# AdaLN attention with a mixture-of-experts FFN on one core: the last unit's chain ordered by hand among the rounds of the group before it, and one copy of k issued later

## The reference

```
x: (2, 1024, 128) f32; 16 heads of 8; one shared k and v of 8 columns; 16 experts, top 4
sa, ca, ga, sb, cb, gb = six slices of silu(c) @ wmod, per batch
h = layernorm(x) * (1 + ca) + sa
x = x + ga * (softmax(causal(q k^T / sqrt(8))) v) @ w_proj      # q, k, v = h @ w_attn
h = layernorm(x) * (1 + cb) + sb
g = sigmoid(h @ gate_w^T); combine = the top 4 of g, divided by their sum, 0 elsewhere
hin, vin = h @ e_win[e], h @ e_vin[e]           # 16 experts of width 64
routed = sum_e (silu(hin) * vin * combine[e]) @ e_wout[e]
shared = (silu(h @ ws_in) * (h @ vs_in)) @ ws_out
x = x + gb * (shared + routed)
```

## Time and profile before

| | us |
|---|---|
| median of 3 runs | 406.76 (405.55 to 408.6) |
| the profiled execution, its own time | 406.49 |
| its span, first to last instruction | 404.8 |
| PE busy | 368.9 (91%) |
| DVE busy | 276.9 (68%) |
| ACT busy | 226.1 (56%) |
| POOL busy | 92.1 (23%) |

### The profile page before, as it was taken

One profiled execution on the slowest core, in us unless ns is written; L12 is line 12 of the kernel. 1 busy time (PEld: TensorE's weight loads), 2 busy tenths in 40 slices (PEclk: granted clock), 3 DMA queues, 4 the chain that ended last, 5 costly groups with the idle time before them and its releaser, 6 DMA issues.

```text
span 404.8 us, 6101 instructions
## 1 busy us (share of the span) xinstructions
PE 368.9 (91%) x2137; PEld 179.2 (44%) x2137; DVE 276.9 (68%) x665; ACT 226.1 (56%) x409; POOL 92.1 (23%) x123
## 2 busy tenths in 40 slices
PE   7978989699999998999899999999979999888965
PEld 7753334334472443436444332334623543254544
DVE  4699755999959989854578366998588880131652
ACT  1312567457587553537753386766856554789231
POOL 6239103604101395003260000042054000000000
PEclk9896799999999998999999999999999999999998
DMA  8540144012305300340110000000080000004000
GB/s 197 116 120 16 53 95 139 24 30 51 80 2 126 88 2 0 102 112 26 34 47 2 1 28 1 2 2 0 5 207 3 0 2 2 27 2 130 30 0 26
DMA packets 24157, 19.46 MB, mean 48 GB/s; under 512 B 7152, under 2 KB 20880, under 8 KB 24128
## 3 DMA queue, kind: packets, MB, share of 16 engines
q1 hardware_dynamic: 23712, 18.69, 18.5%
q10 hardware_dynamic: 416, 0.39, 0.3%
HBM read 11.22 MB, written 1.17 MB: 31 GB/s over the span
## 4 chain that ended last, share of the span: by engine, by line
PE 68%; DVE 21%; ACT 5%; issue 4%; POOL 2%; POOLq 0%; DVEq 0%; ACTq 0%
PE bank L955 63%; DVE mn L834 12%; DVE sl L945 2%; PE bank L1131 1%; ACT pr L682 1%; PE bank L992 1%; DVE shift L846 1%; ACT L682 1%; ACT L686 1%; PE bank L1039 1%; DVE q_left L811 1%; DVE stat L872 1%; DVE q_left L799 0%; DVE xn L759 0%; POOL rstd L557 0%
## 5 line engine op out<-in xcount | busy, mean ns | idle before, releaser
L682 ACT ACTIVATE pr<-bank 128x512 f32<-128x512 f32 x288 | 161.2, 600 | 110.3 <-PE bank L955 109.1
L834 DVE TENSOR_REDUCE mn<-bank 128x1 f32<-128x512 f32 (+3 forms) x304 | 185.3, 653 | 38.3 <-PE bank L955 37.6
L955 PE MATMUL bank<-ka,qa 96*128 96x128 bf16 (+3 forms) x576 | 109.8, 282 | 10.6 <-DVE mn L834 7.1
L955 PE MATMUL bank<-qa,ka 98*128 98x512 bf16 x288 | 108.5, 389 | 1.7 <-ACT pr L682 1.0
L955 PE MATMUL bank<-pr,va 128*32 128x512 f32 x576 | 78.5, 617 | 0.0
L955 PEld LDWEIGHTS bank<-ka,qa 96*128 96x128 bf16 x576 | 46.7, 99 | 61.7 <-DVE mn L834 30.1
L955 PEld LDWEIGHTS bank<-qa,ka 98*128 98x128 bf16 x288 | 27.9, 100 | 80.9 <-ACT pr L682 43.2
L955 PE MATMUL bank<-hT_parts,up_parts 128*128 128x512 f32 (+1 forms) x216 | 61.3, 412 | 1.2 <-ACT sl L686 1.1
L631 POOL TENSOR_TENSOR sl<-sl,comb_wide 128x512 f32<-128x512 f32 x24 | 29.9, 1278 | 75.0 <-DMA comb_wide<-comb_rows 43.9
L955 PEld LDWEIGHTS bank<-hT_parts,up_parts 128*128 128x128 f32 x216 | 38.6, 190 | 12.1 <-issue 2.7
L945 DVE TENSOR_TENSOR sl<-sl,bank 128x512 f32<-128x512 f32 (+1 forms) x36 | 23.4, 651 | 23.4 <-PE bank L955 19.8
(11 more groups left out here) (140 smaller groups left out, 266.9 us busy)
## 6 DMA issues: line engine op xcount, KB each, us to landing
comb_wide<-comb_rows SPq DMA_DIRECT2D x24, 256.0 KB, 5.3
qa<-q_marks SPq DMA_DIRECT2D x4, 768.0 KB, 5.6
qa<-qp SPq DMA_DIRECT2D x18, 128.0 KB
comb_wide<-comb_rows SPq DMA_DIRECT2D x8, 192.0 KB, 3.9
xs<-in_L_attn_x SPq DMA_DIRECT2D x4, 256.0 KB, 4.1
qa<-qp SPq DMA_DIRECT2D x12, 64.0 KB
out_x<-xs SPq DMA_DIRECT2D x3, 256.0 KB, 2.3
sl<-in_L_ffn_e_win SPq DMA_DIRECT2D x1, 512.0 KB, 3.9
```

The costliest lines, as they stand in the source:

```text
L682: act.activation(pr[:, n % NPB, g, :], s_bank[in_s[x] % NS][:, :], ACT.Exp, scale=SCALE).then_inc(s_read, 1)
L834: v.tensor_reduce(mn[:, place[u] % 2, part, h:h + n], m_bank[k % NM][:, 0:n * w].rearrange("p (n w) -> p n w", w=w), AX.X, ALU.max, negate ...
L955: return pe.matmul(out, lhsT, rhs, start=start, stop=stop, skip_group_check=True)
```

## The change

The planner's branch for END and the loop at the end are gone. The end of the list is now written out. Let a round be `gate`, `vin` and `down` of the block before. Of the rounds of LAST, 1 and 2 stand within the last scores as before, and round 3 behind them as before. Then `oT`, round 4, `yT`, `proj`, `norm2`, round 5, `h2`, `h2_split`, `route`, the four `pick`, `up_end` 0 to 4, round 6, `turn_end` 0, round 7, `turn_end` 1 and 2, `down_end`, round 8, `down` 8, `gated`, `turn`. So the output of unit 15 is finished ahead of that of LAST. The gates 1 to 5 of LAST go to POOL, and 6 to 8 stay on DVE. The `k_set` of the third chunk is due 18.0 behind its `k`, not 5.2.

```
@@ then(x) @@
-        elif kind == "h2":
-            plan.extend([("h2_split", a), ("route", a)])
...
-            plan.extend([("up_end", 0), *(("pick", a, i) for i in range(4)), *(("up_end", i) for i in range(1, EP))])
-            plan.extend([("down", LAST, FC), ("gated", LAST), ("turn_end", 0), ("turn", LAST)])
-            plan.extend([*(("turn_end", i) for i in range(1, ET)), ("down_end",)])
...
-            side.append((now + 5.2, ("k_set", a)))
+            side.append((now + (18.0 if a == CHUNKS[2] else 5.2), ("k_set", a)))
@@ the end of the list @@
-    smalls.append((st["now"] + 1.0, ("oT", order[-1])))
-    while side or smalls or vins or st["down"]:
-        step(0.9 if st["down"] else 0.3)
...
+    left = [f for f in range(1, FC + 1) if ("vin", LAST, f) not in plan]
+
+    def rounds(n):
+        for f in left[:n]:
+            if ("gate", LAST, f) not in plan:
+                plan.append(("gate", LAST, f))
+            plan.extend([("vin", LAST, f), ("down", LAST, f - 1)])
+        del left[:n]
+
+    u = order[-1]
+    rounds(1)
+    plan += [("oT", u)]
+    rounds(1)
+    plan += [("yT", u), ("proj", u), ("norm2", END)]
+    rounds(1)
+    plan += [("h2", END), ("h2_split", END), ("route", END)]
+    plan += [*(("pick", END, i) for i in range(4)), *(("up_end", i) for i in range(EP))]
+    rounds(1)
+    plan += [("turn_end", 0)]
+    rounds(1)
+    plan += [("turn_end", 1), ("turn_end", 2), ("down_end",)]
+    rounds(len(left))
+    plan += [("down", LAST, FC), ("gated", LAST), ("turn", LAST)]
...
+    vector_gates = [("gate", LAST, f) for f in range(FC // 2 + 2, FC + 1)]
@@ gpsimd @@
-                elif kind == "gate" and x[1] != LAST:
+                elif kind == "gate" and x not in vector_gates:
...
-                    gp.tensor_tensor(sl[:, f, :], sl[:, f, :], comb_wide[:, f - 1, :], ALU.mult).then_inc(gated_up, 1)
+                    gp.tensor_tensor(sl[:, f, 0:w], sl[:, f, 0:w], comb_wide[:, f - 1, 0:w], ALU.mult).then_inc(gated_up, 1)
@@ vector @@
-                elif kind == "gate" and x[1] == LAST:
+                elif kind == "gate" and x in vector_gates:
```

More of the change, by code:

```diff
@@ L285, in adaln_attention_moe_kernel @@
     plan += [("pv", len(blocks) - 1), ("evac", order[-1])]
-    smalls.append((st["now"] + 1.0, ("oT", order[-1])))
-    while side or smalls or vins or st["down"]:
-        step(0.9 if st["down"] else 0.3)
[L289 to L296, removed]
+    assert {x[1][:2] for x in side + smalls + vins} <= {("gate", LAST), ("vin", LAST)} and not st["down"]
+    left = [f for f in range(1, FC + 1) if ("vin", LAST, f) not in plan]
[19 more added lines that the diff above has]
+    plan += [("down", LAST, FC), ("gated", LAST), ("turn", LAST)]
     kinds = ("cond", "gates", "hT", "q", "k", "v", "oT", "yT", "proj", "h2", "route", "combT", "turn",
@@ L314, in adaln_attention_moe_kernel @@
     in_m = {x: n for n, x in enumerate(x for x in plan if x[0] in ("max", "shift", "vin", "up_end"))}
-    gate_no = {x: n for n, x in enumerate(x for x in plan if x[0] == "gate" and x[1] != LAST)}
+    vector_gates = [("gate", LAST, f) for f in range(FC // 2 + 2, FC + 1)]
+    gate_no = {x: n for n, x in enumerate(x for x in plan if x[0] == "gate" and x not in vector_gates)}
     norms = [x for x in plan if x[0] in ("norm", "norm2")]
@@ L626, in _ @@
                     split(hT_parts[:, k, 0, :], hT_parts[:, k, 1, :], hT[:, c, :], h2_parts)
-                elif kind == "gate" and x[1] != LAST:
+                elif kind == "gate" and x not in vector_gates:
                     c, f = x[1:]
+                    w = width[c]
                     gp.wait_ge(comb_in[c][(f - 1) // SPREAD], 16 * EC)
                     gp.wait_ge(s_read, in_s["hin", c, f] + 1)
-                    gp.tensor_tensor(sl[:, f, :], sl[:, f, :], comb_wide[:, f - 1, :], ALU.mult).then_inc(gated_up, 1)
+                    gp.tensor_tensor(sl[:, f, 0:w], sl[:, f, 0:w], comb_wide[:, f - 1, 0:w], ALU.mult).then_inc(gated_up, 1)
         @block.scalar
@@ L938, in _ @@
                         v.wait_ge(s_read, in_s["hin", c, f] + 1)
-                    elif c == LAST:
-                        v.wait_ge(gated_last, f)
+                    elif ("gate", c, f) in vector_gates:
+                        v.wait_ge(gated_last, vector_gates.index(("gate", c, f)) + 1)
                     else:
```

## The result

The changed kernel is slower: 412.62 us against 408.52, medians of 20 runs each, a ratio of 1.010. I had forecast no change at 406.4, in a range of 404.2 to 408.8; 406.76 times the ratio is 409.6, outside. The loss is under the 1% that the prediction took as what a measurement can tell, but the interval excludes no change.

The account below looks back on a forecast made before the run. PE, 91% busy, was taken as the bound, other steps mattering only where PE waits. Span 404.8 - 1.26 (copy) + 0.5 (tail) + 0.7 (clock) = 404.7, with 1.69 around it 406.4 us; range 404.2 to 408.8.

Parts of the forecast that it names:

- the copy of k: Around 73 us: moving two DVE copies gives back 1.66 and costs 0.40 at the new place, sum -1.26 us.
- the end: Unit 15's chain and the tail to the span's end: the reordered list costs +0.5 us at the full clock.
- -3.78: End of down_end: 398.25 against 402.03, from an earlier start and 2.1 us at the full clock in place of 3.65.
- 4.25: Behind down_end: LAST's chain now stands there, 7.0 us against 2.77, so +4.25.
- a wait that the copy covered: Bound of the copy term: 0 instead of -1.26 us if such a wait comes up in the copy's place.
- Rival C: The copy's gain is taken back by a late maximum or DMA of q marks: 407.7 us; chance 0.11.
- the hold of xn behind gate 5: Unit 15's xn on DVE is held until POOL's gate 5 ends: +0.6 us, bounds 0 and +1.0.
- The clock in up_end: TensorE at 1.2 GHz when the up_end products run: +0.7 us, bounds 0 and +1.2.
- the emptier gap: PE from 383.3 to 386.6, with 0.65 us of work: emptier than before two earlier falls, so the clock falls.
- D: Rival: PE's banks, not the order, held proj, so unit 15's chain is not shortened: 409.5 us; chance 0.05.
- A: Rival: the clock falls a second time and down_end starts at 1.2 GHz: 408.4 us; chance 0.20.
- B: Rival: no hold of xn, no fall of the clock, and the copy gives 1.66: 404.7 us; chance 0.22.

Follow-up runs that it names:

- e1: The kernel before with only the copy of k late (18.0, not 5.2); ratio to before 1.0015 (0.9982 to 1.0048).
- e2: The changed kernel with the copy of k at its old place (5.2): new end and POOL gates alone; ratio to before 1.0061 (1.0022 to 1.0099).
- e8: The kernel before with only POOL's second w_split waiting for the shift, copies of k at their old place; ratio to before 0.9968 (0.9933 to 1.0002).
- e4: The kernel before with the late copy of k and POOL's second w_split waiting for the shift, old end kept; ratio to before 0.9949 (0.9919 to 0.9979).
- e10: e8 with gates 1 to 5 of LAST on POOL, old order kept; executed once for the trace, no ratio, end 24.85 us.
- e11: The changed kernel with POOL's second w_split waiting and gate 5 set ahead of unit 15's norm2; executed once, no ratio, end 26.31 us.
- e3: The changed kernel with POOL's second w_split waiting until DVE has made the shift of unit 9; ratio to before 1.0031 (1.0001 to 1.0061).
- e5: e3 with all eight gates of LAST on POOL, ahead of norm2 of unit 15; ratio to before 0.9977 (0.9946 to 1.0007).
- e6: e3 with round 8, down 8, gated and turn of LAST set ahead of down_end; ratio to before 0.9994 (0.9963 to 1.0025).
- e7: The changes of e5 and e6 together, with rounds 4 to 8 spread; ratio to before 0.9866 (0.9825 to 0.9908), median 402.43 us.
- e9: The changed kernel again, unaltered, timed beside before; ratio to before 1.0046 (1.0012 to 1.0079).

## Why the prediction was wrong

Two terms of the sum failed, the copy of k and the end. Against the forecast, and not against before, the copy's is the larger: it was put at -1.26, and e1 has +0.6 (-0.7 to +2.0). The end and its clock were put at +0.5 and +0.7, and e2 has +2.5 (0.9 to 4.0). With the end alone wrong, the time would still have come out within the range.

**The end: the step that failed is the sum behind it, "-3.78 + 4.25 = +0.5".** The 4.25 was right (behind `down_end` stand 7.21 us, and 7.0 was predicted). The -3.78 had two parts: `down_end` starts 2.24 earlier, and it takes 2.1 in place of 3.65. I gave the second part, 1.55 us, to the new order. The runs show that the old order can do without the slow row too: `down_end` takes 2.17 us in four of its five traces. I saw that the earlier trace rows showed the lower clock, and weighed where the clock would be in the new order, but took the old side from its one trace as if it always fell there. With 24.88 as the old end, the walk gives 24.88 + 0.5 + 1.55 = 26.9, and 26.92 was measured. The end costs 2.0 us where the clock is full in both, and 3.0 where it falls in `up_end` in both. The 2.0 are most of the 2.8 us that a ratio of 1.0069 makes, and e2 shows the end alone at 1.0061.

**The copy of k: "-1.26" was wrong in its step "a wait that the copy covered", which I had as a bound only.** The copies do go and cost the 0.4 at their new place. What I did not ask is what DVE reaches next once it is 1.6 us early. It is a cast of 16 columns, and POOL's second subtraction had just begun. The trace of before had the sign, as its cast took 0.49 us there; my rows end just ahead of it. At the full clock the stretch gave 0.08 (20.57 against 20.65) in place of 1.66, so the term comes to +0.3, and where the clock falls to +2.3. My bound of 0 was too narrow for both. Rival C named the taking back but not the place. With POOL's second split out of the way the same move gives 0.7 in the stretch (e8 to e4, 19.35 to 18.62), or 0.3 with its price at the new place; the wait alone gives 1.3.

**Gates on POOL: right.** Gates 1 to 4 cost nothing (e10), and the hold of xn behind gate 5 was predicted at 0.6 and measured at 0.62 by e11. The Trainium skill, in "SBUF — State Buffer", "Who interferes with whom", has `tensor_scalar` meet GpSimd in a two-port mode only. From the speed of xn I took it that it is in none, and left room for a price of 0. That was my inference and not the page's, which gives the mode as the condition and not a speed. The trace decides: xn took 0.93 beside POOL's gate and 0.35 without it, so the page isn't contradicted, and no run shows the mode.

**The single steps of the chain: right.** After the shift of 8.31, `proj` is at 381.74 (predicted the same), xn ends at 385.10 (385.05), `up_end` starts at 386.68 (386.58), `turn_end` 0 and 1 at 392.10 and 394.46 (392.1 and 394.65), `down_end` starts at 395.81 (396.14).

**The clock in up_end, "+0.7": wrong as a difference.** It fell there in e3 alone of eight traces with unit 15's `proj` early (after, e2, e3, e5, e6, e7, e9, e11), and in three of five with the old order. I had argued that the emptier gap makes the fall sure. In the changed kernel PE was busy 0.69 of 3.31 us in it and the clock held:

```profile
391.68:394.99 3.31, 0.69 (x3) 0.43 (x3) 1.96 (x4) 0.55 (x2) 1.57 (x3) 1.00 0.00 0
```

**The rivals.** None came out as written. D's 409.5 lies nearest to 409.6, by luck: the `proj` row refutes its mechanism. A's 408.4 has the sign right by a wrong mechanism too, as `down_end` ran at the full clock in every trace of the new order. B was right that `up_end` runs at the full clock in most traces, but xn was held, and the copies' removal gave 0.08 and not 1.66. C named what happened to the copy's gain, with a maximum or a DMA in the place of the cast.

**Evac 13 to 14: the clock, at a place that no edit aimed at.** This stretch takes 31.2 us in before and e2, 32.5 to 33.7 in ten other traces, and 34.5 in the changed kernel's first. The granted clock tells them apart. Between 298 and 322 us it stays at 1.00 in before and e2, is at 0.50 for three to four us in the ten, and for about seven in the last. Before, then the changed kernel:

```profile
309.00:310.00 1.00, 1.00 (x7) 0.31 (x4) 0.77 (x3) 0.22 (x1) 0.00 (x0) 1.00 0.00 0
...
309.00:310.00 1.00, 0.93 (x3) 0.38 (x4) 1.00 (x3) 0.00 (x0) 1.00 (x1) 0.50 0.00 0
```

Ahead of it POOL's gates of the third chunk hold the small DVE instructions of the shift one after the other (two of them in before and in e4, three in the changed kernel's first trace). Before and e2 are also the two traced kernels that have both the copies and POOL's split as they were. If the fall hung on that, the late copy and the wait would cost 1.3 us and more here. The ratios speak against it: the other stretches give e8 1.3 and e4 1.6 us, such a price would leave about nothing of either, and e8 and e4 gain 1.3 and 2.1. e4's interval (0.9 to 3.3 us) excludes a gain of nothing and e8's (-0.1 to 2.7) doesn't, so this is argued and not shown.

**What stays open.** Why the clock falls in one trace of a place and not in another, and how often it does at each, as every list of instructions but one was traced once. The falls between evac 13 and 14 alone blur a span by 1.3 to 3.3 us, which is why the ratios of many runs, and not spans, carry the verdicts. In the changed kernel's first trace the start to evac 3 is 2.15 us longer than in before (1.3 in e2, 1.1 in e9, 0.2 in e3 and none in e11, which have the same list there), and that wasn't taken apart.

## What to carry to other kernels

When an instruction is moved away, ask what its engine reaches next in the time that it gains, and what the other engines are doing then; a 16-column cast can cost 2 us. Look too at what the old trace shows at that instruction: a cast already held for 0.3 us there says that something else sets its end. Before a slow row of the old profile is credited to a change, ask whether it belongs to the old order or to that execution: a row at half the PE clock is worth pricing at both clocks on both sides. And a chain that is brought forward over work that used to fill its waits has only swapped which tail is last, unless that work finds another wait to fill.

## What the runs showed of the hardware

- A DVE cast of 16 columns (0.17 us in e4) took 1.99 us beside a POOL subtraction of 2.35 us and ended 0.02 us behind it; a maximum that reads PSUM, next to it on the same engine, kept its 0.6 us beside the same POOL work. In before, the cast that came later took 0.49 us and ended 0.03 us behind the same subtraction.
- The same `tensor_scalar` of 128 columns took 0.34 us alone and 0.93 beside a POOL product of 0.99 us, and ended 0.08 us behind it.
- `down_end` in the old order took 3.65 us at a granted clock of 0.50 and 2.17 at 1.00, with the same instructions around it. PE was busy 0.69 of 3.31 us ahead of the changed kernel's `up_end`, and the clock stayed at 1.00; it was busy 1.64 of 3.40 us ahead of before's `down_end`, and the clock fell to 0.50.
